# Diagonal blocks of 16 instead of 8 in the chunk inverse, one link paired with the corner, and the attention work regrouped into five visits

## The reference

```python
def step(S, inp):                                  # 32 chunks, one after the other
    A_i, v_i, wk_i, rkg_i, wkg_i, intra_i = inp    # A = inv(eye - A0), 64x64, unit lower triangular
    v_new = A_i @ v_i - (A_i @ wk_i) @ S
    o_i = rkg_i @ S + intra_i @ v_new
    S = gamma_C * S + wkg_i @ v_new
    return (S, o_i)

h = _layernorm(x) * (1 + ca) + sa
x = x + ga * attention(h)                          # x: (4, 2048, 256) float32, 4 heads of 64
h = _layernorm(x) * (1 + cb) + sb
x = x + gb * ffn(h)                                # 256 -> 1024 (gated) -> 1024 -> 1024 -> 256
```

## Time and profile before

| | us |
|---|---|
| three runs | 1739.83, 1740.42, 1742.86 |
| median | 1740.42 |
| the profiled execution | 1740.73 |
| its span | 1738.9 |
| TensorE busy | 1709.6 |
| VectorE busy | 1115.6 |
| ScalarE busy | 965.3 |
| GpSimd busy | 593.6 |

### The profile page before, as it was taken

One profiled execution on the slowest core, in us unless ns is written; L12 is line 12 of the kernel. 1 busy time (PEld: TensorE's weight loads), 2 busy tenths in 40 slices (PEclk: granted clock), 3 DMA queues, 4 the chain that ended last, 5 costly groups with the idle time before them and its releaser, 6 DMA issues.

```text
span 1738.9 us, 60528 instructions
## 1 busy us (share of the span) xinstructions
PE 1709.6 (98%) x25488; PEld 1644.4 (95%) x25488; DVE 1115.6 (64%) x3041; ACT 965.3 (56%) x2249; POOL 593.6 (34%) x694
## 2 busy tenths in 40 slices
PE   8799999999999999999999999999999999999999
PEld 5699999999999999999999999999999999999998
DVE  5777666666676666676666676666666666666432
ACT  4664555555555555555555555555555555565554
POOL 3544333243333243333243333243333243243111
PEclk8799999999999999999999999999999999999999
DMA  8201000000000000000000000000000000000000
GB/s 284 76 14 33 12 23 23 18 20 14 22 23 24 19 19 14 21 23 24 17 21 16 19 23 24 17 20 19 16 23 23 19 19 20 15 23 17 8 3 12
DMA packets 37356, 47.08 MB, mean 27 GB/s; under 512 B 9236, under 2 KB 29336, under 8 KB 37080
## 3 DMA queue, kind: packets, MB, share of 16 engines
q1 hardware_dynamic: 35088, 40.75, 8.5%
q10 hardware_dynamic: 1992, 2.38, 0.5%
HBM read 22.53 MB, written 8.39 MB: 18 GB/s over the span
## 4 chain that ended last, share of the span: by engine, by line
PE 93%; DVE 2%; issue 1%; POOL 1%; ACT 0%; DVEq 0%; POOLq 0%
PE mlp L1147 64%; PE mlp L1219 6%; PE solo L1147 3%; PE duo L1415 3%; PE solo L1288 3%; PE solo L1120 2%; PE duo L1336 1%; PE duo L1113 1%; PE duo L1404 1%; PE duo L1108 1%; PE duo L1309 1%; PE solo L1424 1%; PE solo L1130 1%; PE duo L1406 1%; PE duo L1300 1%
## 5 line engine op out<-in xcount | busy, mean ns | idle before, releaser
L1147 PE MATMUL mlp<-act_hi,w_hi 128*128 128x256 f32 x4096 | 967.7, 282 | 1.1 <-POOL act_lo L652 0.6
L1147 PE MATMUL mlp<-act_lo,w_hi 128*128 128x256 f32 x4096 | 945.1, 277 | 0.2
L1147 PEld LDWEIGHTS mlp<-act_hi,w_hi 128*128 128x128 f32 x4096 | 769.8, 188 | 10.1 <-POOL act_lo L652 1.3
L1147 PEld LDWEIGHTS mlp<-act_lo,w_hi 128*128 128x128 f32 x4096 | 770.1, 188 | 1.5 <-issue 0.6
L789 ACT ACTIVATE full<-mlp,scale_sb 128x256 f32<-128x256 f32 x512 | 246.2, 481 | 553.6 <-PE mlp L1147 553.4
L879 DVE TENSOR_TENSOR act_lo<-full,act_hi 128x256 fp32r<-128x256 f32 x512 | 240.2, 469 | 322.6 <-ACT act_hi L790 320.5
L652 POOL TENSOR_TENSOR act_lo<-full,act_hi 128x256 fp32r<-128x256 f32 x256 | 186.6, 734 | 496.0 <-ACT act_hi L779 496.0
L790 ACT ACTIVATE act_hi<-mlp,scale_sb 128x256 fp32r<-128x256 f32 x512 | 243.4, 475 | 0.0
L1147 PE MATMUL mlp<-xh,w_hi 128*128 128x256 f32 x768 | 186.4, 283 | 3.0 <-issue 2.4
L1147 PE MATMUL mlp<-xl,w_hi 128*128 128x256 f32 x768 | 185.4, 281 | 0.0
L591 POOL TENSOR_TENSOR rstd<-ve,minus_half 128x2 f32<-128x2 f32 x64 | 49.0, 766 | 334.2 <-DVE ve L828 334.0
(11 more groups left out here) (179 smaller groups left out, 2675.8 us busy)
## 6 DMA issues: line engine op xcount, KB each, us to landing
w_raw<-in_wts SPq DMA_DIRECT2D x22, 512.0 KB, 5.1
kg<-r SPq DMA_DIRECT2D x64, 126.0 KB
xin<-in_x SPq DMA_DIRECT2D x62, 128.0 KB
out_y<-y SPq DMA_DIRECT2D x62, 128.0 KB, 2.5
step_and_inv<-square_t SPq DMA_DIRECT2D x56, 64.0 KB, 2.0
wmod_sb<-in_wmod ACTq DMA_DIRECT2D x1, 1024.0 KB, 9.5
kg<-last SPq DMA_DIRECT2D x64, 2.0 KB
last<-r SPq DMA_DIRECT2D x64, 2.0 KB, 1.7
```

The lines of the kernel that those rows point to most:

```text
L1147: mm = pe.matmul(dst, *general_ops, start=is_first and i == 0, stop=is_last and i == 1)
```

## The change

What it does:

- `SB` goes from 8 to 16. The substitution (`fs`) has 15 rows, in six parts `FS_ROWS`; it now runs from the last row up, and its shuffles read `low`, not `sub`. `sub_rows` uses the memory of `near`.
- With two blocks of 16 in 32 rows, the inverse needs `first_term` and one more link, `inverse_turned`. `square_and_term`, `n` 3, `first_part` and `step_part`'s second instruction go. VectorE makes `one_less` (identity less the product), ScalarE widens it to `step_wide`. `inverse_turned` is paired with `corner` in `join`, tile by tile.
- `corner` uses 64x64 tiles (`mi` is widened with zeros) instead of 32x32.
- `start` goes behind `state`, for the chunk after next, with `solo` banks for its results; ScalarE makes both copies from PSUM, VectorE none. `gram` goes behind `attn_out`. `near` and `cross` become items of their own on POOL; `intra` goes into the first layer; `far` and `diag` move.
- The last product pair of `l3` 0 is issued behind the first three pairs of `l3` 1 (`BETWEEN`).

```diff
-SB = 8
+SB = 16
 FS = SB - 1
+FS_ROWS = {1: (15, 14), 2: (13, 12), 3: (11, 10), 4: (9, 8), 5: (7, 6, 5), 6: (4, 3, 2, 1)}
+BETWEEN = 3
...
-    mixed = listed([("rg", 0, 0), ("start", 0, 1)], late + layers[:2 * HK], {
-        ("l3", 0): [("norm2", 0, 0)],
-        ("l3", 1): [("values", 0, 1), ("pred", 0, 0), ("gram", 0, 1), ("turn", 0, 0), ("intra", 0, 1), ("u", 0, 0)],
-        ("l3", 2): [("fs", 0, 1)],
-        ("l3", 3): [("fs", 1, 1)],
-        ("l3", 4): [("fs", 2, 1)],
-        ("l3", 5): [("ln2", 0, 0), ("fs", 3, 1)],
+    mixed = listed([("rg", 0, 0), ("fs", 0, 1), ("norm2", 0, 0)], late + layers[:2 * HK], {
+        ("l3", 0): [("fs", 1, 1)],
+        ("l3", 1): [("values", 0, 1), ("pred", 0, 0), ("turn", 0, 0), ("fs", 2, 1), ("u", 0, 0)],
+        ("l3", 2): [("fs", 3, 1)],
+        ("l3", 3): [("fs", 4, 1)],
+        ("l3", 4): [("fs", 5, 1)],
+        ("l3", 5): [("ln2", 0, 0), ("fs", 6, 1)],
         ("l3", 6): [("ln2", 1, 0), ("expand", 0, 1)],
         ("l3", 7): [("parts", 0, 0), ("silu", 0, 0), ("y", 0, 0), ("y", 1, 0)],
-        ("l1", 7): [("lead", 0, 0), ("far", 0, 1), ("stats", 0, 2)],
+        ("l1", 1): [("intra", 0, 1)],
+        ("l1", 2): [("intra", 1, 1)],
+        ("l1", 7): [("lead", 0, 0), ("stats", 0, 2), ("step", 0, 1)],
         ("l2", 0): [("old", 0, 0), ("norm", 0, 2)],
-        ("l2", 1): [("keys", 0, 0)],
-        ("l2", 2): [("join", 0, 0), ("square", 0, 2)],
-        ("l2", 3): [("length", 0, 2)],
-        ("l2", 4): [("n", 3, 1), ("state", 0, 0)],
-        ("l2", 5): [("unit", 0, 2)],
-        ("l2", 6): [("attn_out", 0, 0), ("residual", 0, 2)],
+        ("l2", 1): [("far", 0, 1), ("keys", 0, 0), ("square", 0, 2)],
+        ("l2", 2): [("join", 0, 0), ("length", 0, 2)],
+        ("l2", 3): [("diag", 0, 1), ("unit", 0, 2)],
+        ("l2", 4): [("state", 0, 0), ("start", 0, 2)],
+        ("l2", 6): [("near", 0, 2), ("attn_out", 0, 0), ("gram", 0, 2), ("cross", 0, 2), ("residual", 0, 2)],
     })
...
     second = listed([], layers[:2 * HK], {
-        ("l1", 0): [("fs", 2, 0)],
-        ("l1", 2): [("fs", 3, 0)],
+        ("l1", 0): [("fs", 3, 0)],
+        ("l1", 1): [("fs", 4, 0)],
+        ("l1", 2): [("fs", 5, 0)],
+        ("l1", 3): [("fs", 6, 0)],
         ("l1", 4): [("expand", 0, 0), ("far", 0, 0)],
...
+            def widen(a):
+
+                act.wait_ge(step_ready, a + 1)
+                after(act, inverse_full, a)
+                for i in range(2):
+                    ins = act.activation(step_wide[:, :, HB * i:HB * (i + 1)], one_less[:], ACT.Copy, scale=con[:, CO_BLK + i:CO_BLK + i + 1])
+                ins.then_inc(wide_ready, 1)
...
             def step_part(a):
+                dve.wait_ge(const_in, 16)
                 dve.wait_ge(step_full, a + 1)
-                dve.tensor_copy(step_nt[:].rearrange("p k n -> p (k n)"), duo[0][:, 0, 0:2 * NP * HB])
-                dve.transpose(step_n.rearrange("p k n -> p (k n)"), duo[0][:, 0, 0:2 * NP * HB]).then_inc(step_ready, 1)
+                dve.tensor_tensor(one_less[:], con[:, CO_UNIT:CO_UNIT + HB].unsqueeze(1).to_broadcast([P, 2 * NP, HB]),
+                                  of_head(duo[0][:, 0, 0:2 * NP * HB]), ALU.subtract).then_inc(step_ready, 1)
...
-                        for j in (2 * k - 1, 2 * k):
-                            dve.wait_ge(const_in, 16)
-                            dve.wait_ge(sub_ready[j - 1], now)
-                            dve.stream_shuffle(sub_row[:], sub[:], [i // SB * SB + j for i in range(HB)]).then_inc(term_ready[j - 1], 1)
-                            dve.wait_ge(term_ready[j - 1], 2 * now - 1)
-                            dve.tensor_tensor(sub_term[:], sub_row[:], low[:, :, j:j + 1].to_broadcast([P, 2 * NP, SB]), ALU.mult).then_inc(term_ready[j - 1], 1)
-                            dve.wait_ge(term_ready[j - 1], 2 * now)
-                            dve.tensor_tensor(sub[:], sub[:], sub_term[:], ALU.subtract).then_inc(sub_ready[j], 1)
+                        for j in FS_ROWS[k]:
+                            ins = dve.stream_shuffle(rows[j], low[:, :, 0:j], [i // SB * SB + j for i in range(HB)])
+                        ins.then_inc(rows_ready, 1)
+                        dve.wait_ge(rows_ready, FS_PARTS * a + k)
+                        for j in FS_ROWS[k]:
+                            term = sub_term[:, 0:2 * NP * j].rearrange("p (m n) -> p m n", n=j)
+                            dve.wait_ge(sub_ready, SB * a + SB - j)
+                            dve.tensor_tensor(term, rows[j], sub[:, :, j:j + 1].to_broadcast([P, 2 * NP, j]), ALU.mult).then_inc(term_ready, 1)
+                            dve.wait_ge(term_ready, FS * a + SB - j)
+                            dve.tensor_tensor(sub[:, :, 0:j], sub[:, :, 0:j], term, ALU.subtract).then_inc(sub_ready, 1)
...
-            def square_and_term(m, rows):
-
-                return pe.matmul(duo[1][rows, 0, :].rearrange("p (t k n) -> p t k n", t=2, n=HB)[:, :, m, :], step_nt[rows, m, :],
-                                 step_and_inv[rows, :, m, :], start=True, stop=True)
+            def inverse_turned(m, c, to):
+
+                return pe.matmul(of_head(duo[1][half(to), 1, 0:2 * NP * HB])[:, m, :], step_wide[half(c), m, :],
+                                 inv_t[half(c), m, :], start=True, stop=True)
...
-                return pe.matmul(solo[1][quarter(c, 1), q * P + DH * e:q * P + DH * e + DH], mi[quarter(c, 0), m, :],
-                                 vn[quarter(c, 0), q, e, :], start=False, stop=True, skip_group_check=True)
+                return pe.matmul(solo[1][half(c), q * P + DH * e:q * P + DH * e + DH], mi[half(c), m, :],
+                                 vn[half(c), q, e, :], start=False, stop=True, skip_group_check=True)
...
+                    if paired and k == 0:
+                        layer("l3", 0, range(HK - 1))
+                    if paired and k == 1:
+
+                        layer("l3", 1, range(BETWEEN))
+                        layer("l3", 0, range(HK - 1, HK))
+                        layer("l3", 1, range(BETWEEN, HK))
```

## The result

The changed kernel takes 1802.65 us (median of 4 runs, 1799.78 to 1804.11) against 1740.4 us: ratio 1.0357, 95% interval 1.0345 to 1.037. Forecast were 1767.5 us and at most 1792. The direction was right; the loss is 62 us and not 27.

The account below looks back on a forecast made before the run. TensorE's instruction stream was taken to bound the kernel. From 1740.7 us, 28 x (-0.46 + 1.15) = +19.3, then +8 outside the steady steps and -0.5 for the tail, gave 1767.5 us, range 1732 to 1792.

Parts of the forecast that it names:

- TensorE's sum, -0.46 us a step: TensorE's visits in the steady step: regrouping them shortens its instruction stream by 0.46 us a step.
- rival E: Gram behind attn_out: its tiles cost nothing extra, 9.5 us less in all; shares the 0.50 chance of the main forecast.
- VectorE's walk, +1.15: VectorE's queue from layer 3's column 0: y_mid[0] comes at 22.3, TensorE wants it at 21.13, loss 1.15 us a step.
- three catches: VectorE beside GpSimd's two base instructions and rg: each holds up one VectorE instruction, so the substitution starts at 6.86.
- rival D: VectorE: mask loads drain or xn is late for turn, stall 2.1 us, start +10, 1796 us; chance 0.15.
- Rivals B and C: VectorE beside GpSimd: one instruction caught, 1735 us, chance 0.18; or half caught, stall 0.43 us, 1747 us, chance 0.17.
- Queues at nothing: Work and waits added on ScalarE, VectorE and SP: each priced at nothing.
- The widening: ScalarE ahead of the Gelu table load: first Gelu 0.8 us later, layer 2's column 2 loses 0, bound 0.1.
- Outside the steady steps, +8: First three steps: +1, +3 and +4 us for later inverses and crowded queues, sum +8, bounds 3 and 13.
- Tail: The end, outside the steady steps: 0.5 us shorter.

Follow-up runs that it names:

- all_late: Changed kernel with GpSimd's cross and base later, SP's inverse move first, ScalarE's widening behind old, 11 idle products before the first inverse: 1758.56 us.
- before_more: Kernel before with 18 small VectorE multiplications, whose results nothing waits for, added in each steady step: 1816.72 us.
- few_rows_step_late: Changed kernel with 8 of 15 substitution rows left out in every step and ScalarE's widening behind old: 1731.32 us.
- pool_sp_late: Changed kernel with GpSimd's cross and base instructions behind layer 3's column 7 and SP's inverse move ahead of the attention loads: 1763.25 us.
- idle_all: Changed kernel with 11 instead of 4 idle TensorE products before the first inverse, and more at waits in the second and third step: 1797.12 us.
- pool_late: Changed kernel with GpSimd's cross and two base instructions moved behind layer 3's column 7 of the next step: 1793.93 us.
- few_rows: Changed kernel with 8 of the 15 substitution rows left out in every step, so the inverse is incomplete: 1740.45 us.

## Why the forecast was too small

**TensorE's sum, -0.46 us a step.** The steps of this working held. A visit measured as before (from the last product ahead of it to the second behind it, less two slots) is 2.19 for lead, 1.27 for join (forecast 1.27), 2.12 for state with start (1.27 + 0.88 - 0.05), 2.55 for attention output with gram (1.72 + 0.47 + 0.34), 2.94 for the rest: 11.07 against 11.50 us, -0.43. Gram's tiles are not free (rival E): without the 0.34 the visit of attention output with gram would be 2.19, and it is 722.54 - 719.75 = 2.79, less 0.235:

```profile
719.75 0.28 PE L1170 MATMUL mlp<-act_lo,w_hi 128*128 128x256 f32 x1
...
721.69 0.70 PE L1335 MATMUL duo<-rT 64*64 64x65 f32 x32
...
722.54 0.28 PE L1170 MATMUL mlp<-act_lo,w_hi 128*128 128x256 f32 x1
```

Yet the step with both new waits removed (all_late) is only 0.10 us shorter than before in the median and 0.03 in the mean (51.99 and 52.02). I had priced visits and assumed that all else between them stays what it is: the pace of the FFN products and the rare waits of the earlier trace rows. That is the failed step, and neither stayed.

The pace: products leave every 0.1135 us or every 0.118. Between 240 and 1560 us 19% of them leave at the slower one before, 38% after, 35% in all_late. The rise has one place. Behind the turn, through the last six columns of layer 3 and on into y, products have the slower pace in every second step and the faster one in the step between, in the kernel after and in each of its eleven variants. In the kernel before and in before_more they have the faster one there in every step. The chain that ended last in all_late, four consecutive steps, answers the earlier trace rows:

```profile
606.61 10.90 PE mlp L1170 x96
...
657.92 11.31 PE mlp L1170 x96
...
709.68 10.90 PE mlp L1170 x96
...
761.77 11.31 PE mlp L1170 x96
```

By the counts all_late pays (0.35 - 0.19) x 336 products x 0.0044 = 0.24 us a step for it. The slower pace comes with the change, since no variant is without it; which part of the change brings it is open.

The rare waits: 8.6 us in 27 steps in all_late, 2.9 in the earlier trace rows, 0.21 us a step. few_rows_step_late has the same pace and only 1.6 us of them, and its mean step is 51.74, 0.28 us below the kernel before. So 0.28 of the 0.46 us is what was left of the gain where no engine held TensorE up. In all_late -0.43 + 0.24 + 0.21 makes +0.02, and -0.03 was measured; against the -0.46 forecast this term is short by 0.43 us a step.

**VectorE's walk, +1.15.** Mechanism and place were right: three catches, a shuffle at 7.02 (6.86), then no rest. Sizes: the six parts took 10.43 us and not 10.1, the last low half was issued at t = 20.93 (20.4), layer 1 began at 22.85 where it wanted to at 21.13. From that low half to y_mid it took 1.77 us; the 1.87 of the forecast should have been 1.91 by its own rows, a slip that changes nothing. TensorE stops twice and pays each restart. By pool_sp_late this term is 53.66 - 52.36 = 1.30 in the mean (1.54 in the median): short by 0.15. The mask loads were free (two shuffles with their masks start 0.20 us apart at 731.25 us), the reduce that writes 128 values took 1.07 us, so rival D's mechanism fell, though its time, 1796 us, was the nearest; that is luck. Rivals B and C needed a catch less than three; there is none less.

**Queues at nothing.** The widening was the wrong one of these: 0 forecast, bound 0.1, measured 52.36 - 51.99 = 0.37. The forecast had 0.8 us go ahead of the table load and left 0 to 0.05 us to spare; it was 0.91 us of widening and the wait of 0.26 for one_less, which the forecast did not have, and column 2 then paid the lateness and a restart. Intra, unit, ScalarE's copies of start and SP's move show no wait.

Together 0.43 + 0.15 + 0.37 = 0.95 us a step, the difference between +0.69 and +1.64, and 26 us in all. The three are differences between mean steps of one profile each, and rare waits of 0.1 to 0.4 us a step are in these means.

**Outside the steady steps, +8, measured +18.1.** The waits were counted, and the count came out near: I had +1 for the first step, which came to 2.3, and +7 for the second and third, where idle_all leaves 8.3. The step that failed here is that no term stood for the clock: TensorE slows after it waits, 7.5 us. The profile of before had the clue: its clock is 0.83 up to the first turn and 0.90 in the first leg. The upper bound of 13 had no term for it. Tail: -0.9 (-0.5).

## What to carry to other kernels

Before work is added to an engine with slack, walk its queue from the deadline back, with what the shared engine next to it catches; here three GpSimd instructions at the wrong moment (cross and the two base) cost as much as eight rows of substitution, and moving them took back about 40 of 62 us. When such an instruction is moved, look at who waits for its result in another queue: SP's wait for base held up an inverse it had nothing to do with. And long waits of TensorE are to be priced twice, once as time and once as products at half clock behind them: here 8.3 and 7.5 us.

## What the runs showed of the hardware

- **The clock.** In the kernel after, the granted clock fell to its lower level (1.2 of 2.4 GHz) at 33.6 us, in the 7.2 us wait for the first inverse, which ended at 37.0, and stayed there until 54.0; again from 81.4 to 91.6, beside two waits of some 1.7 us each, from 132.6 to 139.4, behind one of 3.2, and for 3.4 us each from 176.9 and 187.2. Two windows in these stretches (columns as above, the clock is the third from the end):

```profile
34.00:44.00 10.00, 5.86 (x68) 4.22 (x70) 8.83 (x36) 3.75 (x6) 4.09 (x5) 0.50 0.99 348
...
132.00:139.00 7.00, 6.48 (x53) 6.45 (x54) 6.72 (x16) 1.73 (x4) 3.72 (x4) 0.54 0.01 4
```

  There an FFN product takes almost twice as long, one every 0.21 us, as two rows of TensorE's timeline show:

```profile
86.40 0.41 PE L1170 MATMUL mlp<-act_lo,w_hi 128*128 128x256 f32 x1
86.61 0.41 PE L1170 MATMUL mlp<-act_hi,w_hi 128*128 128x256 f32 x1
```

  Seven more idle products at the first wait and 39 in four other places (idle_all) removed these stretches but for 3.4 us from 52.4, with no other change. It is not a matter of the start alone: in pool_late the clock is at its lower level for 3.4 us from 277.3 us, in a steady step, behind a wait of 3.8 us for the moved inverse. This agrees with the Trainium skill (TensorE: Matmul & The Clock Gate, What's actually happening): "the default state is throttled, and activity releases the throttle".
- **Two paces of one product.** The same 128x256 product leaves every 0.1135 us or every 0.118 at the upper clock level: 96 of them take 10.90 or 11.31 us in the rows of all_late above. Long runs begin behind a visit or a wait and keep their pace through layer 3 and y (127 products at 0.118 in one step of few_rows, 126 at 0.1135 in the step before); within layer 1 it can change without a gap. In the changed kernel the pace behind the turn goes with the parity of the step. What decides is open.
- **Restarts.** Behind a wait, of 1.5 us as of 0.15, the second product comes 0.19 to 0.23 us behind the first and not 0.12. So short waits cost more than their length.
